# The constant of a recurrence as the bias column of its tanh, and bias rows as products over all 128 rows

## The chip, the cores and the metric

One NeuronCore of a Trainium2 chip runs the whole kernel. The metric is the device time of one execution in microseconds (us), the median of the runs shown. TensorE (PE) multiplies matrices, VectorE (DVE), ScalarE (ACT) and GpSimd (POOL) do the rest, and SyncE (SP) issues the DMAs.

## What is computed

The reference is two decoder layers on x of shape (8, 256, 128). What matters here is the second layer's state-space part and what comes right behind it:

```python
u  = einsum('bsd,nd->bsn', x, Wi) + bi
sp = einsum('bsd,nd->bsn', x, Ws) + bs
def step(state, inp):
    u_t, sp_t = inp
    state = tanh(state @ A.T + u_t @ B.T) + sp_t
    return (state, state @ C.T)
out = einsum('bsn,dn->bsd', ys, Wo) + bo        # ys: 256 steps, one after the other
x = layernorm(x + out)
x = layernorm(x + cross_attention(x, ctx))      # linear attention; its last step: att @ dense_w + dense_b
```

The first layer (local self-attention, cross-attention with rotary keys, a quantized product) comes before it and takes three quarters of the time. The last step of all is a quantized product with a normalization.

## The kernel before

**The recurrence.** The kernel keeps h_t = tanh(...) in place of the state. All batches are in one tile of 8 columns, so a step is `z_t = A h_(t-1) + (B Wi) x_t + (A Ws) x_(t-1) + constant`, then a tanh of 128 x 8. The part without h is put into PSUM (`cf`, four banks, 2048 columns) ahead of its step: the first 512 columns by `z_of` (L1776), the other 1536 in 12 blocks of 128 columns by `z_third` (L1791), one third of a block in each of the steps 1 to 36. The three thirds of a block are the product with x_t (`bwi_t`, L1798), the product with x_(t-1) (`aws_t`, L1801), and the constant (L1804). The constant is a row: `c_rows`, one partition of 256 values, multiplied by a row of ones (`one_row`, one partition), which puts the constant into every column. A product of one row is a matmul that contracts over one partition. In the trace its shape reads 1*64 (one row, 64 columns of weights), where the others read 128*64.

**A step.** On PE, `step(t)` (L1807) waits for `h_ready`, adds `A h` into the step's 8 columns by two matmuls of 64 output partitions each (L1810; an f32 matmul shows as two records, so one step shows as four) and raises `z_ready`. On ACT, `step(t)` (L900) waits for it, computes the tanh (L902, the first one L899) and raises `h_ready`. So the 256 steps are a chain that alternates between the two engines.

**What is woven in.** PE's instructions stand in one written-out order. Behind the matmuls of step t comes the work of `window(k, i)` (L1862) with k, i = divmod(t, 16): what the later parts need, cut into pieces of about one product. With 16 steps to a window of 128 tokens, piece 0 is `inputs_of`: the product with `gws_t` into `bank_d` and then the bias row (`one_row` times `bias_row`). Piece 1 is `states_of`, 2 to 5 the attention of an earlier window (`attend`, products of 16 columns), 6 is `dense` with its own bias row (`one_row` times one partition of `b_dense`), 7, 8, 11 and 15 are turns (L1818), 9 a product. `product_of_rows` (L1821) makes each as two halves of 64 partitions; its records are all on L1823, told apart by their operands: `x_t,sin_t` is `bias_row` with `one_row`, `b_dense,sin_t` the dense one. Where a step has no such piece, `keep_clock` (L1747) multiplies 192 columns (96 while there are thirds) that nobody reads.

**The small products.** Before the recurrence, PE makes the weight products (L1727 to L1738), among them the constants as rows of one partition: L1730, and L1735 to L1738, whose weights are single columns of `cols`. DVE copies them out (L1224, L1227, L1228). The tiles `bias_row`, `one_row` and `c_rows` are rows of `x_t`, `sin_t` and `rec_t`, free by then; POOL fills `one_row` at L681.

**The end.** SP's queue carries, for each window, a store of x4 and of the attention and a reload of the latter (L517, L521, L524), and behind those of window 13 eight loads (L531), then the rest for windows 14 and 15 and eight more loads (L535). The last sums on DVE wait for the loads.

Of the kernel before, what the change touches and what calls it, by code (L numbers as in the profile page):

```python
# [24 lines left out]
ACT = mybir.ActivationFunctionType  # L25
AX_X = mybir.AxisListType.X

B, T, D = 8, 256, 128
S = 512
P = 128  # L30
# [112 lines left out]
Z_FIRST = 512  # L143
Z_PARTS = (T * B - Z_FIRST) // P
# [3 lines left out]
KEEP, KEEP_Z = 192, 96  # L148
# [25 lines left out]
def decoder(nc, a, out):  # L174
    with ExitStack() as ctx:
        def sb(name, shape, dt=F32):
            return ctx.enter_context(nc.sbuf_tensor(name, shape, dt))

        def sem(name):
# [117 lines left out]
        x4_rows = bias_mask[:, :, :].rearrange("p h c -> p (h c)")[:, 0:WINDOWS * D].rearrange("p (t d) -> p t d", d=D)  # L297
        bias_row = x_t[0:1, 0:D]
        one_row = sin_t[0:1, :]
        c_rows = rec_t[0:1, 0:2 * D]  # L300
        t4 = cn[:, :, :]
# [3 lines left out]
        (F_MAX, F_SUM, F_ALL, BETA, INV_BETA, F_INV, F_SCALE, OUT_BIAS, Q_MAX, Q_SCALE, Q_INV) = (  # L305
            0, 4, 5, 6, 7, 8, 9, 10, 11, 13, 15)
        diag2 = sb("diag2", [2, 4])
        level = f_all
# [235 lines left out]
        def _(pool):  # L544
# [135 lines left out]
            pool.wait_ge(y_full, B)  # L680
            g.memset(one_row, 1.0).then_inc(ident16_ready, 1)  # L681
            norms = B * SELF_NORMS
# [50 lines left out]
        def _(act):  # L733
# [164 lines left out]
            act.wait_ge(c_ready, 1)  # L898
            s.activation(hid[:, 0:B], cf[:, 0:B], ACT.Tanh).then_inc(h_ready, 1)  # L899
            def step(t):  # L900
                act.wait_ge(z_ready, t)
                s.activation(hid[:, t * B:(t + 1) * B], cf[:, t * B:(t + 1) * B], ACT.Tanh).then_inc(h_ready, 1)  # L902

# [22 lines left out]
        def _(dve):  # L926
# [296 lines left out]
            w.tensor_copy(tail[:, 3:6, :].rearrange("p k d -> p (k d)"), bank_d[:, 0:3 * D])  # L1223
            w.tensor_copy(c_rows[:, 0:D], bank_d[0:1, 3 * D:4 * D]).then_inc(td_free, 1)  # L1224
            dve.wait_ge(td_full, 3)
            w.tensor_tensor(gws_t, bank_d[:, 0:D], ident[:, :], ALU.add)
            w.tensor_copy(c_rows[:, D:2 * D], bank_d[0:1, D:2 * D])  # L1227
            w.tensor_copy(bias_row, bank_d[0:1, 2 * D:3 * D]).then_inc(td_free, 1)  # L1228

# [176 lines left out]
        def _(pe):  # L1406
# [310 lines left out]
            for k in range(4):  # L1717
# [11 lines left out]
            mm(bank_d[:, 2 * D:3 * D], mats[:, M_C, :], wo_t, start=True, stop=True, skip_group_check=True)  # L1729
            mm(bank_d[0:1, 3 * D:4 * D], cols[:, BI_COL:BI_COL + 1], b_t, start=True, stop=True,  # L1730
               skip_group_check=True).then_inc(td_full, 1)

            pe.wait_ge(td_free, 2)
            mm(bank_d[:, 0:D], mats[:, M_WS, :], g_t, start=True, stop=True, skip_group_check=True)
            mm(bank_d[0:1, D:2 * D], cols[:, BI_COL:BI_COL + 1], b_t, start=True, stop=False, skip_group_check=True)  # L1735
            mm(bank_d[0:1, D:2 * D], cols[:, BS_COL:BS_COL + 1], a_t, start=False, stop=True, skip_group_check=True)
            mm(bank_d[0:1, 2 * D:3 * D], cols[:, BS_COL:BS_COL + 1], g_t, start=True, stop=False, skip_group_check=True)
            mm(bank_d[0:1, 2 * D:3 * D], cols[:, BO_COL:BO_COL + 1], ident[:, :], start=False, stop=True,  # L1738
               skip_group_check=True).then_inc(td_full, 1)

# [33 lines left out]
            pe.wait_ge(ta_free, 9)  # L1774
            pe.wait_ge(ident16_ready, 2)
            def z_of(lo, hi, start):  # L1776

                bank = cf[:, lo:hi]
                mm(bank, bwi_t, x3_t[:, lo:hi], start=start, stop=False, skip_group_check=True)
                skip = B if lo == 0 else 0  # L1780
                mm(bank[:, skip:], aws_t, x3_t[:, lo + skip - B:hi - B], start=False, stop=False,
                   skip_group_check=True)
                last = mm(bank[:, skip:], c_rows[:, D:2 * D], one_row[:, skip:hi - lo], start=False, stop=True,
                          skip_group_check=True)
                if skip:
                    last = mm(bank[:, 0:B], c_rows[:, 0:D], one_row[:, 0:B], start=False, stop=True,
                              skip_group_check=True)
                return last

            z_of(0, Z_FIRST, True).then_inc(c_ready, 1)  # L1790
            def z_third(part, third):  # L1791

                lo = Z_FIRST + P * part
                for half in range(0, P, HALF_ROWS):
                    of = slice(half, half + HALF_ROWS)
                    bank = cf[of, lo:lo + P]
                    if third == 0:
                        mm(bank, bwi_t[:, of], x3_t[:, lo:lo + P], start=(lo % 512 == 0), stop=False,  # L1798
                           skip_group_check=True)
                    elif third == 1:  # L1800
                        mm(bank, aws_t[:, of], x3_t[:, lo - B:lo + P - B], start=False, stop=False,  # L1801
                           skip_group_check=True)
                    else:
                        mm(bank, c_rows[:, D + half:D + half + HALF_ROWS], one_row[:, 0:P], start=False, stop=True,  # L1804
                           skip_group_check=True)
# [15 lines left out]
            def product_of_rows(bank, tokens, weights, **kw):  # L1821
                for of in halves:
                    last = mm(bank[of, 0:D], tokens[:, of], weights, skip_group_check=True, **kw)  # L1823
                return last

            def inputs_of(k):
                if k == 0:
                    pe.wait_ge(td_free, 9)
                else:
                    pe.wait_ge(q_ready, k)  # L1830
                product_of_rows(bank_d, x3_t[:, P * k:P * k + P], gws_t, start=True, stop=False)
                product_of_rows(bank_d, one_row[:, 0:P], bias_row, start=False, stop=False)

# [20 lines left out]
            def dense(k):  # L1854
                pe.wait_ge(mixed_t_ready, k + 1)
                if k >= 1:
                    pe.wait_ge(dense_normed, k)
                product_of_rows(bank_d2, mixed_t, w_dense[:, :], start=True, stop=False)
                product_of_rows(bank_d2, one_row[:, 0:P], b_dense[0:1, :], start=False,
                                stop=True).then_inc(dense_full, 1)  # L1860

# [38 lines left out]
            for t in range(1, T):  # L1900
                step(t)
                k, i = divmod(t, WINDOW_STEPS)
                worked = window(k, i)
                if t <= 3 * Z_PARTS:
                    z_third(*divmod(t - 1, 3))
                if not worked:
                    keep_clock(KEEP_Z if t <= 3 * Z_PARTS else KEEP, bank_d2 if t < Z_FIRST // B else sc[:, 0, :])
            pe.wait_ge(h_ready, T)
# [56 lines left out]
```

## Time and profile before

| | |
|---|---|
| median of 3 runs | 1149.36 us (1147.28 to 1156.16) |
| the profiled execution's own time | 1147.91 us |
| its span, first to last instruction | 1146.1 us |
| mean granted clock of TensorE | 0.889 of full speed |
| the recurrence, first tanh (L899) to last | 901.6 to 1075.4 us |
| tanh instructions L902 | 255, each 0.177 us |
| steps 1 to 248, 902.20 to 1070.88 us | 168.68 us, mean granted clock 0.79 |

How to read it: times count from the span's first instruction. The granted clock is 1.00 or 0.50 at any moment (2.4 or 1.2 GHz); a mean between them is a share of time. In a timeline row, the bracket says how long the engine stood idle before, and who released it.

### The profile page before, as it was taken

The page shows a single profiled execution, that of the slowest core. Times are in us where ns is not written, and L with a number is a line of the kernel's source. Part 1 is how long each engine was busy: PE and PEld are TensorE (multiplying, and loading weights), DVE is VectorE, ACT ScalarE, POOL GpSimd, SP SyncE. Part 2 cuts the span into 40 slices and gives each one's busy share as a digit, 9 for nine tenths or more (in the row PEclk, how much of TensorE's full clock was granted, in tenths as well). Part 3 has the DMA queues.
Part 4 walks back from the last instruction along what each step waited for, and adds up shares of the span by engine and source line. Part 5 has one row for each costly group of instructions (what it writes and reads, how often), then busy time and mean ns, then how long its engine had stood idle before and what let it go on. Part 6 is the DMA issues. An engine that isn't in the chain of part 4 may idle for free.

```text
span 1146.1 us, 21485 instructions
## 1 busy us (share of the span) xinstructions
PE 966.1 (84%) x8233; PEld 665.1 (58%) x8233; DVE 682.3 (60%) x1923; ACT 500.3 (44%) x1412; POOL 494.0 (43%) x615
## 2 busy tenths in 40 slices
PE   3658999998999999899899999988844899999811
PEld 2435666666665666666666575655533677677501
DVE  3356676657657766875776777575555123433478
ACT  3636654563564565466456455633310222332200
POOL 1035366356446545644644654566531012222351
PEclk8689999999899999999999999999975877877755
DMA  6000000000000000000000000000000011111400
GB/s 175 20 1 6 11 1 5 11 1 5 2 10 1 5 11 1 6 11 1 1 5 11 2 1 1 2 1 20 1 1 0 4 16 18 20 23 18 54 7 37
DMA packets 60396, 15.06 MB, mean 13 GB/s; under 512 B 41334, under 2 KB 59526, under 8 KB 60166
## 3 DMA queue, kind: packets, MB, share of 16 engines
q1 hardware_dynamic: 60294, 13.69, 6.0%
q8 instruction: 66, 1.08, 0.4%
q14 instruction: 36, 0.29, 0.1%
HBM read 10.51 MB, written 3.17 MB: 12 GB/s over the span
## 4 chain that ended last, share of the span: by engine, by line
PE 61%; DVE 20%; ACT 6%; POOL 5%; issue 3%; SPq 3%; DMA 2%; POOLq 0%; DVEq 0%
PE score_banks L1650 8%; PE out_bank L1622 7%; PE bank_a L1410 5%; PE score_banks L1429 5%; PE score_banks L1810 5%; DVE o_rec L1130 5%; DVE prob L1158 3%; PE score_banks L1454 3%; PE bank_d L1505 3%; PE score_banks L1431 3%; PE out_bank L1605 3%; PE score_banks L1430 3%; PE bank_d L1823 3%; PE out_bank L1630 2%; PE score_banks L1749 2%
## 5 line engine op out<-in xcount | busy, mean ns | idle before, releaser
L851 ACT ACTIVATE prob<-score_banks 128x1024 f32<-128x1024 f32 x128 | 131.0, 1023 | 166.0 <-PE score_banks L1650 165.8
L1650 PE MATMUL score_banks<-qh,kr 64*128 64x256 f32 x1024 | 149.6, 412 | 3.1 <-ACT qh L819 2.7
L664 POOL TENSOR_TENSOR psum<-psum,prob 128x512 f32<-128x512 f32 x64 | 81.6, 1276 | 156.7 <-DVE prob L1158 156.7
L1130 DVE RECIPROCAL o_rec<-out_bank 128x256 f32<-128x256 f32 x64 | 111.9, 1748 | 30.6 <-PE out_bank L1630 30.6
L662 POOL TENSOR_TENSOR psum<-prob 128x512 f32<-128x512 f32 x64 | 83.0, 1297 | 102.6 <-DVE prob L1158 102.6
L1622 PE MATMUL out_bank<-prob,v 128*64 128x256 f32 x1024 | 124.7, 386 | 1.3 <-DVE on L1131 1.3
L1650 PEld LDWEIGHTS score_banks<-qh,kr 64*128 64x128 f32 x1024 | 91.2, 191 | 41.8 <-issue 32.4
L791 ACT ACTIVATE prob<-prob,neg_max 128x128 f32<-128x128 f32 (+1 forms) x256 | 107.1, 426 | 12.9 <-DVE neg_max L1030 12.9
L1158 DVE TENSOR_SCALAR prob<-prob 128x1024 f32<-128x1024 f32 x128 | 101.2, 791 | 18.4 <-ACT prob L851 18.4
L902 ACT ACTIVATE prob<-score_banks 128x8 f32<-128x8 f32 x255 | 45.2, 177 | 121.5 <-PE score_banks L1810 121.5
L1622 PEld LDWEIGHTS out_bank<-prob,v 128*64 128x64 f32 x1024 | 67.8, 136 | 46.6 <-issue 17.2
L1810 PE MATMUL score_banks<-prob,pt 128*64 128x8 f32 x1020 | 89.7, 228 | 1.8 <-ACT prob L899 0.3
L1810 PEld LDWEIGHTS score_banks<-prob,pt 128*64 128x64 f32 x1020 | 68.1, 163 | 38.8 <-ACT prob L902 27.1
L1092 DVE TENSOR_TENSOR k_cos<-score_banks,cos_t 128x512 f32<-128x512 f32 x56 | 38.2, 682 | 82.1 <-PE score_banks L1431 45.9
L640 POOL TENSOR_TENSOR kr<-k_cos,k_sin 128x512 f32<-128x512 f32 x64 | 82.8, 1294 | 8.8 <-DVE k_sin L1094 8.7
L666 POOL TENSOR_TENSOR psum<-psum,prob 128x512 f32<-128x512 f32 x64 | 81.5, 1273 | 3.9
L1505 PE MATMUL bank_d<-km,q 64*128 64x128 f32 (+1 forms) x512 | 57.4, 346 | 24.4 <-DVE row_max L1025 21.0
L742 ACT ACTIVATE pt<-bank_a 128x512 f32<-128x512 f32 x96 | 57.3, 597 | 42.9 <-PE bank_a L1410 41.8
L690 POOL TENSOR_TENSOR var_eps<-mv,epsilons 128x1 f32<-128x1 f32 x48 | 9.1, 189 | 149.8 <-DVE mv L1276 149.8
L1410 PE MATMUL bank_a<-ident,prob 128*128 128x128 f32 x384 | 62.3, 286 | 11.6 <-ACT pt L742 5.4
L1410 PEld LDWEIGHTS bank_a<-ident,prob 128*128 128x128 f32 x384 | 43.1, 142 | 33.5 <-ACT pt L742 17.6
L1505 PEld LDWEIGHTS bank_d<-km,q 64*128 64x128 f32 x512 | 37.3, 203 | 40.8 <-issue 39.0
(340 smaller groups left out, 2114.3 us busy)
## 6 DMA issues: line engine op xcount, KB each, us to landing
cb<-in_ctx_dram SPq DMA_DIRECT2D x8, 256.0 KB, 2.8
bias_mask<-bias_scratch SPq DMA_DIRECT2D x1, 1536.0 KB, 7.4
xb<-in_x_dram SPq DMA_DIRECT2D x8, 128.0 KB, 2.1
prob<-in_L_xattn_Wkv_dram SPq DMA_DIRECT2D x1, 1024.0 KB, 7.1
x_scratch<-v SPq DMA_DIRECT2D x16, 64.0 KB, 1.5
att_scratch<-on SPq DMA_DIRECT2D x16, 64.0 KB, 1.5
prob<-att_scratch SPq DMA_DIRECT2D x16, 64.0 KB, 2.9
out_dram<-v SPq DMA_DIRECT2D x4, 256.0 KB, 2.5
```

Of the source, the lines that this page charges most:

```text
L640: g.tensor_tensor(kr[:, key % 2, :], k_cos[:, :], k_sin[:, :], ALU.add).then_inc(kr_ready, 1)
L662: link(g.tensor_tensor(psum[:, p % 2, :], pp[:, 0, :], pp[:, 1, :], ALU.add))
L664: link(g.tensor_tensor(psum[:, p % 2, :], psum[:, p % 2, :], pp[:, 2, :], ALU.add))
L791: last = s.activation(pr, pr, ACT.Exp, bias=neg_max[:, qt, j, g:g + 1], accum_out=row_sum[:, qt, j, g:g + 1])
L851: s.activation(prob[:, p % 2, 2 * u:2 * u + 2, :].rearrange("p k (h q) -> p h k q", h=2), sc[:, 0:2, :].rearrange("p h (k q) -> p h k q", ...
L1130: link(w.reciprocal(o_rec[:, :], bank[:, T:2 * T]))
L1158: w.tensor_scalar(pr, pr, float(np.exp(-CLIP)), float(np.exp(CLIP)), ALU.max, ALU.min).then_inc(clamped, 1)
L1410: return nc.tensor.transpose(out_ap, in_ap, ident[0:in_ap.shape[0], 0:in_ap.shape[0]])
L1505: last = mm(bank[:, lo:lo + k.stop - k.start], q0[rows_of, q], km[rows_of, jj, k], start=True, stop=True, skip_group_check=True)
L1622: mm(o[DH * h:DH * (h + 1), 0:T], v[:, (q // 2) % 2, kb, lo:lo + DH], prob[:, q % 2, kb, T * h:T * (h + 1)], start=(kb == 0), stop=(kb == ...
L1650: last = mm(sc[:, h, k * T:(k + 1) * T], kr[rows_of, p % 2, kb * P:(kb + 1) * P], qh[rows_of, p % 2, :], start=True, stop=True, skip_group ...
L1810: last = mm(cf[lo:lo + HALF_ROWS, t * B:(t + 1) * B], a_t[:, lo:lo + HALF_ROWS], hid[:, (t - 1) * B:t * B], start=False, stop=True, skip_g ...
```

## The change

The constant of the recurrence is no longer multiplied into PSUM. It is kept as a column of 128 values (`z_bias`: one column for the first step, one for the others), made by products with one moving column, and given to the tanh as its bias. The thirds become halves: 12 blocks in the steps 1 to 24, `keep_clock` with 192 columns from step 25 on. The two bias rows of the side work stay products, but over all 128 rows: `first_row` is a 128 x 64 tile whose first partition is ones and the rest zeros; `pre_bias` holds the bias row on all 128 partitions (its weights are a column broadcast over 128 columns), and `b_dense` was loaded on all partitions already.

```diff
-        bias_row = x_t[0:1, 0:D]
-        one_row = sin_t[0:1, :]
-        c_rows = rec_t[0:1, 0:2 * D]
+        pre_bias = x_t[:, 0:D]
+        first_row = rec_t[:, 0:HALF_ROWS]
+        z_bias = sb("z_bias", [P, 2])
 ...
             pool.wait_ge(y_full, B)
-            g.memset(one_row, 1.0).then_inc(ident16_ready, 1)
 ...
             act.wait_ge(c_ready, 1)
-            s.activation(hid[:, 0:B], cf[:, 0:B], ACT.Tanh).then_inc(h_ready, 1)
+            act.wait_ge(td_free, 3)
+            s.activation(hid[:, 0:B], cf[:, 0:B], ACT.Tanh, bias=z_bias[:, 0:1]).then_inc(h_ready, 1)
             def step(t):
                 act.wait_ge(z_ready, t)
-                s.activation(hid[:, t * B:(t + 1) * B], cf[:, t * B:(t + 1) * B], ACT.Tanh).then_inc(h_ready, 1)
+                s.activation(hid[:, t * B:(t + 1) * B], cf[:, t * B:(t + 1) * B], ACT.Tanh,
+                             bias=z_bias[:, 1:2]).then_inc(h_ready, 1)
 ...
-            w.tensor_copy(c_rows[:, 0:D], bank_d[0:1, 3 * D:4 * D]).then_inc(td_free, 1)
+            w.tensor_copy(z_bias[:, 0:1], bank_d[:, 3 * D:3 * D + 1])
+            w.tensor_copy(first_row, ident[:, 0:1].broadcast_to([P, HALF_ROWS])).then_inc(td_free, 1)
 ...
-            w.tensor_copy(c_rows[:, D:2 * D], bank_d[0:1, D:2 * D])
-            w.tensor_copy(bias_row, bank_d[0:1, 2 * D:3 * D]).then_inc(td_free, 1)
+            w.tensor_copy(z_bias[:, 1:2], bank_d[:, D:D + 1])
+            w.tensor_copy(pre_bias, bank_d[:, 2 * D:3 * D]).then_inc(td_free, 1)
 ...
-            mm(bank_d[0:1, 3 * D:4 * D], cols[:, BI_COL:BI_COL + 1], b_t, start=True, stop=True,
+            mm(bank_d[:, 3 * D:3 * D + 1], b_t, cols[:, BI_COL:BI_COL + 1], start=True, stop=True,
                skip_group_check=True).then_inc(td_full, 1)
 ...
-            mm(bank_d[0:1, D:2 * D], cols[:, BI_COL:BI_COL + 1], b_t, start=True, stop=False, skip_group_check=True)
-            mm(bank_d[0:1, D:2 * D], cols[:, BS_COL:BS_COL + 1], a_t, start=False, stop=True, skip_group_check=True)
-            mm(bank_d[0:1, 2 * D:3 * D], cols[:, BS_COL:BS_COL + 1], g_t, start=True, stop=False, skip_group_check=True)
-            mm(bank_d[0:1, 2 * D:3 * D], cols[:, BO_COL:BO_COL + 1], ident[:, :], start=False, stop=True,
-               skip_group_check=True).then_inc(td_full, 1)
+            mm(bank_d[:, D:D + 1], b_t, cols[:, BI_COL:BI_COL + 1], start=True, stop=False, skip_group_check=True)
+            mm(bank_d[:, D:D + 1], a_t, cols[:, BS_COL:BS_COL + 1], start=False, stop=True, skip_group_check=True)
+            to_all = [P, P]
+            mm(bank_d[:, 2 * D:3 * D], cols[:, BS_COL:BS_COL + 1].broadcast_to(to_all), g_t, start=True, stop=False,
+               skip_group_check=True)
+            mm(bank_d[:, 2 * D:3 * D], cols[:, BO_COL:BO_COL + 1].broadcast_to(to_all), ident[:, :], start=False,
+               stop=True, skip_group_check=True).then_inc(td_full, 1)
 ...
-                last = mm(bank[:, skip:], c_rows[:, D:2 * D], one_row[:, skip:hi - lo], start=False, stop=True,
-                          skip_group_check=True)
-                if skip:
-                    last = mm(bank[:, 0:B], c_rows[:, 0:D], one_row[:, 0:B], start=False, stop=True,
-                              skip_group_check=True)
-                return last
+                return mm(bank[:, skip:], aws_t, x3_t[:, lo + skip - B:hi - B], start=False, stop=True,
 ...
-                        mm(bank, c_rows[:, D + half:D + half + HALF_ROWS], one_row[:, 0:P], start=False, stop=True,
 ...
+            def bias_of_rows(bank, row, **kw):
+                for of in halves:
+                    last = mm(bank[of, 0:D], first_row, row, skip_group_check=True, **kw)
+                return last
 ...
-                product_of_rows(bank_d, one_row[:, 0:P], bias_row, start=False, stop=False)
+                bias_of_rows(bank_d, pre_bias, start=False, stop=False)
 ...
-                product_of_rows(bank_d2, one_row[:, 0:P], b_dense[0:1, :], start=False,
-                                stop=True).then_inc(dense_full, 1)
+                bias_of_rows(bank_d2, b_dense[:, :], start=False, stop=True).then_inc(dense_full, 1)
 ...
-                if t <= 3 * Z_PARTS:
-                    z_third(*divmod(t - 1, 3))
+                if t <= 2 * Z_PARTS:
+                    z_half(*divmod(t - 1, 2))
                 if not worked:
-                    keep_clock(KEEP_Z if t <= 3 * Z_PARTS else KEEP, bank_d2 if t < Z_FIRST // B else sc[:, 0, :])
+                    keep_clock(KEEP_Z if t <= 2 * Z_PARTS else KEEP, bank_d2 if t < Z_FIRST // B else sc[:, 0, :])
```

## Rows read from the trace of the kernel before

**Rows 1.** The page, part 2: granted clock of TensorE in 40 slices of 28.65 us.

```profile
PEclk8689999999899999999999999999975877877755
```

**Rows 2.** Waits of ScalarE in the recurrence, 901 to 1076 us.

```profile
ACT prob L902 <- PE score_banks L1810: 121.5, 255, 1.3
```

**Rows 3.** Chain that ended last, from 1071 us (start, us, what).

```profile
1074.17 1.04 SPq L531
```

**Rows 4.** Timeline of one step, first weaving part, full clock (start, us, engine ...).

```profile
903.21 0.43 PE L1804 MATMUL score_banks<-sin_t,rec_t 1*64 1x128 f32 x4
903.33 0.18 ACT L902 ACTIVATE prob<-score_banks 128x8 f32<-128x8 f32 x1 [0.39 <-PE score_banks L1810]
...
904.07 0.18 ACT L902 ACTIVATE prob<-score_banks 128x8 f32<-128x8 f32 x1 [0.57 <-PE score_banks L1810]
```

**Rows 5.** Timeline of a side product step at full clock.

```profile
989.86 0.18 ACT L902 ACTIVATE prob<-score_banks 128x8 f32<-128x8 f32 x1 [0.39 <-PE score_banks L1810]
...
990.01 0.43 PE L1823 MATMUL bank_d<-x_t,sin_t 1*64 1x128 f32 x4
...
990.71 0.18 ACT L902 ACTIVATE prob<-score_banks 128x8 f32<-128x8 f32 x1 [0.67 <-PE score_banks L1810]
```

**Rows 6.** Timeline of a side product step at the low clock.

```profile
966.73 0.18 ACT L902 ACTIVATE prob<-score_banks 128x8 f32<-128x8 f32 x1 [0.49 <-PE score_banks L1810]
...
968.19 0.18 ACT L902 ACTIVATE prob<-score_banks 128x8 f32<-128x8 f32 x1 [1.28 <-PE score_banks L1810]
...
968.86 0.18 ACT L902 ACTIVATE prob<-score_banks 128x8 f32<-128x8 f32 x1 [0.49 <-PE score_banks L1810]
```

**Rows 7.** Timeline of step 17: two 128-row products, full clock.

```profile
912.44 0.42 PE L1823 MATMUL bank_d<-pt,prob 128*64 128x128 f32 x4
...
912.64 0.18 ACT L902 ACTIVATE prob<-score_banks 128x8 f32<-128x8 f32 x1 [0.89 <-PE score_banks L1810]
912.69 0.39 PE L1801 MATMUL score_banks<-prob,pt 128*64 128x128 f32 x4
...
913.20 0.18 ACT L902 ACTIVATE prob<-score_banks 128x8 f32<-128x8 f32 x1 [0.39 <-PE score_banks L1810]
```

**Rows 8.** Timeline of two keep-clock steps, low clock.

```profile
930.84 0.18 ACT L902 ACTIVATE prob<-score_banks 128x8 f32<-128x8 f32 x1 [0.68 <-PE score_banks L1810]
...
931.69 0.18 ACT L902 ACTIVATE prob<-score_banks 128x8 f32<-128x8 f32 x1 [0.68 <-PE score_banks L1810]
```

**Rows 9.** Groups of ScalarE by form: mean ns of one, without and with operand columns.

```profile
L742 ACT ACTIVATE ctx_t<-bank_a,cols 128x512 f32<-128x512 f32 x8 | 6.2, 773 | 7.5 <-PE bank_a L1410 7.5
...
L742 ACT ACTIVATE ctx_t<-bank_a 128x512 f32<-128x512 f32 x8 | 4.8, 602 | 0.0
...
L738 ACT ACTIVATE sin_t<-bank_a,sign 128x512 f32<-128x512 f32 x1 | 0.7, 687 | 0.0
```

**Rows 10.** Timeline of the first constants of the recurrence.

```profile
899.43 1.01 PE L1781 MATMUL score_banks<-prob,pt 128*128 128x504 f32 x2
...
901.63 0.18 ACT L899 ACTIVATE prob<-score_banks 128x8 f32<-128x8 f32 x1 [3.22 <-PE score_banks L1786]
```

**Rows 11.** Timeline of the weight products, 858 to 865 us.

```profile
858.96 0.64 PE L1728 MATMUL bank_d<-pt,km 128*128 128x128 f32 x2
...
859.39 0.64 PE L1729 MATMUL bank_d<-pt,km 128*128 128x128 f32 x2
...
861.37 0.80 PE L1734 MATMUL bank_d<-pt,km 128*128 128x128 f32 x2 [0.84 <-DVE rec_t L1224]
...
862.10 0.58 PE L1735 MATMUL bank_d<-pt,cols 128*1 128x128 f32 x2
```

**Rows 12.** Busy time, clock and DMA of three windows of 16 steps.

```profile
989.86:1000.31 10.45, 10.32 (x152) 7.17 (x148) 4.31 (x16) 3.34 (x19) 3.09 (x8) 0.84 0.16 20
1021.01:1032.28 11.27, 11.14 (x150) 8.40 (x148) 4.07 (x16) 3.35 (x20) 3.09 (x8) 0.71 0.16 21
966.73:979.38 12.65, 12.64 (x152) 9.51 (x150) 4.36 (x16) 3.34 (x19) 3.09 (x8) 0.56 0.13 17
```

More of the change, by code:

```diff
@@ L1774, in _ @@
             pe.wait_ge(ta_free, 9)
-            pe.wait_ge(ident16_ready, 2)
+            pe.wait_ge(ident16_ready, 1)
             def z_of(lo, hi, start):
@@ L1780, in z_of, with z_half @@
                 skip = B if lo == 0 else 0
-                mm(bank[:, skip:], aws_t, x3_t[:, lo + skip - B:hi - B], start=False, stop=False,
-                   skip_group_check=True)
-                last = mm(bank[:, skip:], c_rows[:, D:2 * D], one_row[:, skip:hi - lo], start=False, stop=True,
+                return mm(bank[:, skip:], aws_t, x3_t[:, lo + skip - B:hi - B], start=False, stop=True,
                           skip_group_check=True)
-                if skip:
-                    last = mm(bank[:, 0:B], c_rows[:, 0:D], one_row[:, 0:B], start=False, stop=True,
-                              skip_group_check=True)
-                return last
             z_of(0, Z_FIRST, True).then_inc(c_ready, 1)
-            def z_third(part, third):
+            def z_half(part, which):
                 lo = Z_FIRST + P * part
@@ L1796, in z_third @@
                     bank = cf[of, lo:lo + P]
-                    if third == 0:
+                    if which == 0:
                         mm(bank, bwi_t[:, of], x3_t[:, lo:lo + P], start=(lo % 512 == 0), stop=False,
                            skip_group_check=True)
-                    elif third == 1:
-                        mm(bank, aws_t[:, of], x3_t[:, lo - B:lo + P - B], start=False, stop=False,
-                           skip_group_check=True)
                     else:
-                        mm(bank, c_rows[:, D + half:D + half + HALF_ROWS], one_row[:, 0:P], start=False, stop=True,
+                        mm(bank, aws_t[:, of], x3_t[:, lo - B:lo + P - B], start=False, stop=True,
                            skip_group_check=True)
```

## The prediction, made before the changed kernel ran

> **What bounds the kernel now.** I read the page first. The granted clock is nearly full until slice 30 and then 0.5 to 0.8 [rows 1]: something else begins there, at about 900 us, and that is the recurrence, the part that the change touches. Next the waits of ScalarE there. All 255 tanh waited for PE, 121.5 us together [rows 2], and PE's next step waits for the tanh in turn. So neither engine is the bound by its load; a chain through both is, one link per step. In the timeline I took the distance from tanh to tanh in each of the 247 intervals between step 1 and step 248 (168.68 us), and sorted them by what PE had in them:
>
> - 114 plain ones at the full clock, 0.565 us each. PE's side work is hidden: even with two products over 128 rows the interval is 0.56 [rows 7].
> - 54 plain ones at the low clock, 0.666 (968.19 to 968.86 in [rows 6]).
> - 32 at the low clock with `keep_clock` of 192 columns, 0.853 [rows 8]. These are bound by PE, not by the chain.
> - 8 in between (the clock changed in them).
> - 39 with a product of one row. 10 are those of the thirds, 0.747 [rows 4]; steps 16 and 32 take 1.06 and 1.07, steps 33 and 36 0.85 and 0.82. 25 are in `inputs_of` and `dense` from step 48 on: 20 at 0.850 [rows 5], 4 at 1.46 (966.73 to 968.19 in [rows 6]), one of 1.05.
>
> The one-row product costs time though it moves no more columns than the others: 0.285 us more than a plain interval in rows 5, where a second product over 128 rows costs nothing in rows 7.
>
> Last the end of the chain: SP's loads L531 start at 1074.17 [rows 3], behind the attention of window 13, which step 248 carries. From there the chain is SP's and DVE's own. So what happens up to step 248 moves the end one to one, and what happens behind it on PE (the bias rows of the last windows too) is hidden behind SP's eight loads.
>
> **The bias column on the tanh.** It adds no instruction, but each tanh reads a column of SBUF that it did not read before. No row shows a tanh with one. The nearest rows: the same evacuation of 128x512 costs 602 ns with no column, 773 with scale and bias columns, and 687 with a scale column alone [rows 9]. So one column is 85 ns (687 - 602) and two are 171. The row with one column stood alone and waited for PE before it, as the tanh does, so the wait did not hide it. Bounds: 0, if the column is fetched while the instruction waits; 0.11 as the upper end, the price of rows 9 and a quarter more. I take 0.087, what one column costs there (0.085) rounded up. Where the chain bounds, it is paid in full. Where `keep_clock` bounds it is free, since 0.853 - 0.666 = 0.187 covers it. Plain intervals become 0.652 and 0.753.
>
> The Trainium skill says the same against this change. In ScalarE: Activation LUTs, under What ACT_TABLE_LOAD costs, each [128,1] pointer operand adds about 93 ns to an activation with immediates. By that price the sum below would be 1.0 us higher (an estimate: 168 plain intervals times 6 ns); the rows above have the price for other functions and agree within 10%.
>
> **Interval by interval, at the clock pattern of the trace:**
>
> - 114 + 54 = 168 plain, +0.087 each: +14.6.
> - 32 with `keep_clock`: 0. The 8 mixed ones, about +0.04 each: +0.3.
> - Steps 25 to 36 now have `keep_clock` with 192 columns and no third: 0, hidden by the chain while the clock is full, as in the plain ones; 0.1 each (0.853 - 0.753) if the clock falls there.
> - 10 thirds, 0.747 to 0.652: -0.95.
> - Step 16 has two side products and one half, three products. Two take 0.25 us apart (912.44 and 912.69 [rows 7]) and fit 0.56, so three end near 0.8: -0.25. Step 32 no longer has a half: 1.07 to 0.652, -0.4. Steps 33 and 36: -0.35 together.
> - 20 side biases, 0.850 to 0.652 (two 128-row products fit): -4.0.
> - 4 at the low clock. 128 columns take 0.25 at the full clock, so 0.50 here. `keep_clock` with 192 columns makes 0.853 [rows 8]; two products are 256 columns, 64 more, so 0.853 + 0.25 = 1.10 (an estimate). 1.46 to 1.10 is -1.4 for the four, and the mixed one -0.25. The ends are 0.753 (all hidden) and 1.46 (nothing gained), so -2.8 and 0.
>
> Sum: +14.9 - 7.6 = +7.3.
>
> **Ahead of the recurrence.** `z_of` loses its constants: L1781 ends at 900.44, the first tanh started at 901.63 [rows 10]. That is -1.15, and +0.09 for its own bias column. The first tanh's new wait (`td_free` 3) is for copies of the products that ran at about 862 [rows 11], so it is long met, and PE waits for one POOL instruction less. The weight products: two 128-wide ones start 0.43 apart, but the first one-column product starts 0.73 after L1734 [rows 11]. I put that gap down to the change of shape, which goes twice: -0.6. The added copy of `first_row` (64 columns) stands between two links on DVE: +0.1. Range of the two -1.0 to +0.5, since a 128-column load of a broadcast column has no row. POOL's memset goes at a time when POOL next waits for DVE's statistics, which hide it: 0, and if they did not, a gain of under 1 us. Together -1.56.
>
> At the same clock pattern the sum is +7.3 - 1.56 = +5.7 us.
>
> **The clock.** It falls for short stretches in each window, after the attention's 16-column products, and that is dear: a window of 16 steps took 10.45 at a mean clock of 0.84, 11.27 at 0.71, 12.65 at 0.56 [rows 12], so 0.8 us for one low stretch more (10.45 to 11.27). The change pulls both ways. The same columns are spread over longer steps, which would let it fall more often; and the one-row products become products of the whole array, which would let it fall less often. The trace has no row for either. Longer steps are 168 of 247, bias products 25, so I lean to the first: two or three more low stretches, +2. Bounds -3 and +7.
>
> Result: +5.7 + 2 = +7.7 on the profiled execution's own 1147.91 (its span of 1146.1 and 1.8 around it), so 1155.6. The median of the runs is 1.45 above that execution, so 1149.36 + 7.7 = 1157.1.
>
> **The rivals.**
> 1. *The column is fetched during the wait* (faster). Place: each tanh. For it: the instruction is queued well before its data. Against: rows 9. The time: thirds 10 x 0.18, steps 16, 32, 33 and 36 together 1.3, 20 x 0.285, 4 x 0.36 and 0.45 for the mixed one make -10.7; -1.65 ahead of the recurrence; shorter steps with the same columns would also keep the clock up, -2. 1149.4 - 14.3 = 1135.1. It is faster by over 1% up to a column of (14.3 - 11.5) / 168 = 0.017 us.
> 2. *The clock stays down more* (clearly slower). Place: windows 3 to 15, where the attention's small products stand in longer steps; the window at 0.56 shows how far it can go [rows 12]. With eight more low stretches it is 8 x 0.8 = +6.4 in place of +2: 1149.4 + 5.7 + 6.4 = 1161.5. From eight on it is over 1%.
> 3. *The clock gains*, since bias products of the whole array keep it up: three fewer low stretches, -2.5: 1149.4 + 5.7 - 2.5 = 1152.6.
> 4. *The one-row penalty does not go*: if it came from adding a bias to a bank that was just written and not from the row count, the steps keep 0.85 + 0.087. Against it: a third's constant (another bank, other operands) is late in the same way [rows 4]. The 25 side steps would lose their gain again, 25 x 0.285: 1149.4 + 5.7 + 7.1 = 1162.2.
>
> **How the numbers follow.** A measurement of this kernel can tell about 1% (11.5 us) from no change. Forecast 1157.1: 0.45. Rival 1: 0.13. Rival 2: 0.22. Rival 3: 0.15. Rival 4: 0.05. Faster by over 1% is rival 1, 0.13. Slower by over 1% is rivals 2 and 4 and a tail of the forecast, 0.29. The rest, 0.58, is within 1%, most of it above the old time. The range for 8 in 10 reaches from rival 3 with part of a cheaper column, 1145, to rival 2 with a column of 0.1, 1167.
>
> **What would show it.** In the changed profile: tanh rows of about 0.264 us, not 0.177; plain intervals 0.65; no shape 1*64, and side bias steps at the full clock equal to plain ones; the low-clock ones near 1.10; the first tanh 1.1 us after L1781's place, not 2.2. Tanh rows of 0.177, or intervals of 0.565 in spite of a longer tanh, would make the forecast wrong and rival 1 right. A mean clock below 0.75 over the recurrence would be rival 2, above 0.82 rival 3.

## The result and the profile after

| | before | changed |
|---|---|---|
| median of 15 runs each | 1149.67 us (1140.25 to 1156.16) | 1158.43 us (1155.05 to 1160.11) |
| profiled execution's span | 1146.1 us | 1156.7 us |
| first tanh to step 1's tanh start | 901.63 to 902.20 | 899.60 to 900.25 |
| steps 1 to 248 | 168.68 us, clock 0.79 | 181.36 us, clock 0.75 |

The ratio is 1.0062, with a 95% interval of 1.0039 to 1.0085: slower by 0.4 to 0.9%. The forecast was 1157.1 us.

The page's clock line of the changed kernel answers to [rows 1]. In slices 32 to 38, which lie in the recurrence, it reads 9676777 where it read 8778777. (The first slices differ too, long before anything that was changed.)

```profile
PEclk9979999999999899999999999998965967677755
```

The group of the tanh in the lines by form. It was 177 ns; it reads a third operand now, `z_bias`, and takes 267 ns:

```profile
L902 ACT ACTIVATE prob<-score_banks,z_bias 128x8 f32<-128x8 f32 x255 | 68.2, 267 | 112.3 <-PE score_banks L1805 112.3
```

So the column costs 90 ns in the instruction. What the chain makes of it, in the timeline at a step with a side product and its bias row, at the full clock; it answers to [rows 5], where the interval was 0.85:

```profile
968.26 0.27 ACT L902 ACTIVATE prob<-score_banks,z_bias 128x8 f32<-128x8 f32 x1 [0.39 <-PE score_banks L1805]
968.31 0.39 PE L1823 MATMUL bank_d<-x_t,rec_t 128*64 128x128 f32 x4
...
968.92 0.27 ACT L902 ACTIVATE prob<-score_banks,z_bias 128x8 f32<-128x8 f32 x1 [0.39 <-PE score_banks L1805]
```

The shape 1*64 is gone, the bias row reads 128*64, and the interval is 0.66, which is also what a plain step takes (0.565 before). Plain intervals: about 126 of the 247 at 0.65 or 0.66, and 52 at 0.76 at the low clock (0.666 before). Six with two products at the low clock take 1.07, where [rows 6] had 1.46. One of them in the timeline:

```profile
960.28 0.27 ACT L902 ACTIVATE prob<-score_banks,z_bias 128x8 f32<-128x8 f32 x1 [0.46 <-PE score_banks L1805]
...
960.54 0.65 PE L1823 MATMUL bank_d<-b_dense,rec_t 128*64 128x128 f32 x4
...
961.35 0.27 ACT L902 ACTIVATE prob<-score_banks,z_bias 128x8 f32<-128x8 f32 x1 [0.63 <-PE score_banks L1805]
```

The first constants answer to [rows 10]. The tanh starts 1.05 us behind the start of the product with `aws_t` (L1781 before, L1785 now), where it was 2.20:

```profile
898.55 1.01 PE L1785 MATMUL score_banks<-prob,pt 128*128 128x504 f32 x2
...
899.60 0.27 ACT L899 ACTIVATE prob<-score_banks,z_bias 128x8 f32<-128x8 f32 x1 [2.06 <-PE score_banks L1785]
```

The weight products answer to [rows 11]. The product with one moving column, L1732, starts 0.42 behind L1731, and L1737 0.59 behind L1736 where the one-column weights had needed 0.73. From the sum product (L1724 before, L1726 now, at 857.70 and 857.36) to DVE's next reduction it took 6.91 us before (864.61) and takes 6.37 now:

```profile
859.05 0.63 PE L1731 MATMUL bank_d<-pt,km 128*128 128x128 f32 x2
...
859.47 0.42 PE L1732 MATMUL bank_d<-cols,pt 128*128 128x1 f32 x2
...
860.72 0.80 PE L1736 MATMUL bank_d<-pt,km 128*128 128x128 f32 x2 [0.82 <-DVE rec_t L1226]
...
861.31 0.42 PE L1737 MATMUL bank_d<-cols,pt 128*128 128x1 f32 x2
...
863.73 0.68 DVE L1234 TENSOR_REDUCE small<-prob 128x1 f32<-128x512 f32 x1
```

Two windows of 16 steps, and steps 1 to 248 as a whole, with TensorE's clock behind the bracketed counts; they answer to [rows 12]. Nearly all windows from step 80 on take 11.70 and 12.20 by turns, with the same places at the low clock each time, while before they varied from 10.3 to 12.65:

```profile
956.06:968.26 12.20, 11.60 (x152) 8.62 (x152) 4.44 (x16) 4.78 (x19) 3.07 (x8) 0.70 0.13 17
968.26:979.96 11.70, 11.00 (x150) 7.86 (x148) 4.16 (x16) 4.78 (x19) 3.09 (x8) 0.73 0.14 18
900.25:1081.61 181.36, 172.40 (x2300) 125.85 (x2298) 58.53 (x203) 72.72 (x288) 39.24 (x104) 0.75 0.12 17
```

A mean clock of 0.75 says how long the low clock held: 2 x (1 - 0.75) x 181.36 = 91 us; before, with 0.79, it was 71. The clock is read to two decimals, so such a figure is good to about 2 us.

And the end, SP's first load L531, answers to [rows 3]. It starts 10.73 us later than before, which is the whole difference of the spans (10.6); nothing was gained or lost behind it:

```profile
1084.90 1.05 SPq L531
```

### The profile page after: what moved, and what is told of

Read it like the earlier page. It is cut to its first block, busy times and chain, and to the rows that moved or that the text cites. A ratio compares the mean times of both kernels' runs of the same rounds, so it can differ in the third digit from the quotient of the medians.

```text
span 1156.7 us, 21383 instructions
## 1 busy us (share of the span) xinstructions
PE 970.0 (84%) x8181; PEld 668.8 (58%) x8181; DVE 682.5 (59%) x1924; ACT 523.1 (45%) x1412; POOL 493.1 (43%) x614
## 4 chain that ended last, share of the span: by engine, by line
PE 61%; DVE 19%; ACT 8%; POOL 4%; issue 3%; SPq 3%; DMA 2%; POOLq 0%; DVEq 0%
PE score_banks L1652 9%; PE out_bank L1624 7%; PE score_banks L1805 5%; PE bank_a L1412 5%; PE score_banks L1431 5%; DVE o_rec L1131 4%; DVE prob L1159 3%; PE score_banks L1456 3%; PE bank_d L1507 3%; PE score_banks L1432 3%; PE score_banks L1433 3%; PE out_bank L1607 3%; PE score_banks L1753 2%; PE out_bank L1632 2%; ACT prob L902 2%
## 5 line engine op out<-in xcount | busy, mean ns | idle before, releaser
L902 ACT ACTIVATE prob<-score_banks,z_bias 128x8 f32<-128x8 f32 x255 | 68.2, 267 | 112.3 <-PE score_banks L1805 112.3
```

## The experiments

Two theories stood against each other after the result. **Theory:** the column is paid on the chain, the rows are saved on PE, and both prices are those of the intervals plus what they do to the clock. **Rival:** the clock alone makes the difference, or the saving of the rows isn't there. The two parts of the change are taken apart first, then the clock is held.

### e1: the column alone

```diff
+            act.wait_ge(td_free, 3)
+            s.activation(hid[:, 0:B], cf[:, 0:B], ACT.Tanh, bias=z_bias[:, 0:1]).then_inc(h_ready, 1)
...
+                s.activation(hid[:, t * B:(t + 1) * B], cf[:, t * B:(t + 1) * B], ACT.Tanh,
+                             bias=z_bias[:, 1:2]).then_inc(h_ready, 1)
...
+            w.memset(z_bias[:, :], 0.0)
```

> The kernel before with one thing added: each tanh gets a bias column, which is zero (a DVE memset makes it). Theory (the column costs about 0.09 us in every step whose interval the chain sets): tanh rows of 0.267 us; plain intervals 0.656 at the full and 0.757 at the low clock; the intervals with keep_clock at the low clock stay 0.853 and those with a one-row side product 0.85, because PE sets them. 168 x 0.09 = +15, and 2 to 4 more by low clock: 1149.7 + 18 = 1168. Rival (the time of the changed kernel comes from the clock alone, and the column is fetched beside the chain): the same within 3 us of before, 1150.

Measured: 1182.95 us (1180.54 to 1184.70), ratio 1.0298 (1.0262 to 1.0335). The group of its tanh (the 230 that ran before 1090 us), and a window of 16 steps with steps 1 to 248:

```profile
L904 ACT ACTIVATE prob<-score_banks,z_bias 128x8 f32<-128x8 f32 x230 | 61.6, 268 | 119.4 <-PE score_banks L1814 119.4
```

```profile
974.25:988.23 13.98, 13.98 (x150) 10.03 (x150) 4.28 (x16) 4.78 (x20) 3.10 (x8) 0.50 0.12 15
902.55:1104.21 201.66, 197.94 (x2348) 140.08 (x2346) 58.31 (x203) 72.81 (x288) 39.65 (x104) 0.64 0.11 15
```

The row of the tanh is as the theory had it, and so are the intervals: 0.656 at the full clock, 0.753 to 0.760 at the low one, 0.853 with `keep_clock`, and 0.85 for one-row steps. But the total is 33.3 above before, not 18. The clock is why: it is 0.64 over steps 1 to 248, 145 us at the low clock in place of 71, and six of the windows are wholly at 0.50 and take 13.98. The rival falls. The theory's direct price stands, and its price for the clock (2 to 4 us) was far too small.

### e2 and e3: the rows without the column

e2 is the changed kernel with the tanh's column off (it leaves out the constant):

```diff
-                s.activation(hid[:, t * B:(t + 1) * B], cf[:, t * B:(t + 1) * B], ACT.Tanh,
-                             bias=z_bias[:, 1:2]).then_inc(h_ready, 1)
+                s.activation(hid[:, t * B:(t + 1) * B], cf[:, t * B:(t + 1) * B], ACT.Tanh).then_inc(h_ready, 1)
```

> The changed kernel with the bias column taken off the tanh, all else as changed (it leaves out the constant of the recurrence). Theory: plain intervals back to 0.565 and 0.666, side steps at the full clock 0.565 too; 10.7 us saved in the steps, 2 ahead of them, 2 by the clock: 1149.7 - 14.7 = 1135. Rival (the clock alone): as the changed kernel, 1158.

e3 computes everything. It is the kernel before, with every one-row product made one of 128 rows:

```diff
+            link(g.memset(first_ones[:, :], 0.0))
+            g.memset(first_ones[0:1, :], 1.0).then_inc(ident16_ready, 1)
...
+            mm(bank_d[:, 3 * D:4 * D], cols[:, BI_COL:BI_COL + 1].broadcast_to(to_all), b_t, start=True, stop=True,
...
-                        mm(bank, c_rows[:, D + half:D + half + HALF_ROWS], one_row[:, 0:P], start=False, stop=True,
+                        mm(bank, c_all[:, D + half:D + half + HALF_ROWS], first_ones[:, 0:P], start=False, stop=True,
```

> A version that takes the product over 128 rows for all constants, those of the recurrence too, and leaves the tanh without a column: the thirds stay thirds, their constant is c_all (the constant on all partitions) with a tile whose first partition is ones. Theory: a third's constant hides in the 0.565 of its step as the other two thirds do, so it is as fast as e2 plus about 1 us for the first 512 columns' constant ahead of the recurrence: 1136. Rival (each side product that is left in costs something, whatever its rows): the 12 thirds keep their 0.18, so 1139 or more.

Measured: e2 1126.41 us (ratio 0.9814, 0.9779 to 0.9849), e3 1123.63 us (0.9779, 0.9746 to 0.9812). They are 8.6 and 12.4 below what was expected. A window and the steps 1 to 248 of e3:

```profile
978.34:987.39 9.05, 8.89 (x152) 6.08 (x150) 4.23 (x16) 3.35 (x20) 3.10 (x8) 1.00 0.17 23
903.88:1048.21 144.33, 142.44 (x2348) 106.04 (x2346) 57.61 (x203) 50.63 (x287) 39.29 (x103) 0.93 0.15 21
```

A window in which the clock never falls takes 16 x 0.565 = 9.05, with both bias rows in it: they are hidden wholly. The thirds' intervals are 0.56 and 0.57 in e3, so the rival of e3 falls: a third's constant over 128 rows costs nothing there. Here too the saving is larger than expected (26 us, not 14), and here too it is the clock: 0.93, 20 us at the low clock in place of 71.

### e4: the side products alone

Against e3, the constants of the recurrence (this line, and the two of `z_of`) go back to one row:

```diff
-                        mm(bank, c_all[:, D + half:D + half + HALF_ROWS], first_ones[:, 0:P], start=False, stop=True,
+                        mm(bank, c_all[0:1, D + half:D + half + HALF_ROWS], first_ones[0:1, 0:P], start=False, stop=True,
```

> As e3, but the constants of the recurrence stay products of one row; only the bias rows of the side products (inputs_of, dense) are over 128 rows. It splits the saving. Theory: thirds' intervals 0.747 again, 1.8 us for the ten and 0.8 for steps 18 to 36 with side work, so 1139; the side steps 0.565 at the full clock. Rival (the one-row penalty sits in the thirds alone): 1149.

Measured: 1128.15 us (ratio 0.982, 0.9788 to 0.9853). The thirds' intervals are 0.75 and the side steps 0.565, as the theory had them; the total was expected at 1139 and is 11 below it, with a mean clock of 0.90 over steps 1 to 248. So of e3's 26 us, 21.5 come from the two bias rows per window and 4.5 from the recurrence's own constants.

### e7, e8, e9, e12: the same square with the clock held

If the clock carries so much, then holding it must leave the direct prices. Before it falls PE has the attention's steps, with products of 16 columns only; so these four kernels get a product of 128 columns there that nobody reads (the fill):

```diff
                 worked = window(k, i)
+                if 2 <= i <= 5 and 0 <= k - 2 < WINDOWS and t > 2 * Z_PARTS:
+                    keep_clock(P, bank_d2 if t < Z_FIRST // B else sc[:, 0, :])
```

(3 * Z_PARTS in e8, e9 and e12, which have thirds.)

> The changed kernel, with a keep_clock product of 128 columns added behind each of the attention's steps (pieces 2 to 5) once the halves are through; nobody reads it. It asks how much of the column's price is the clock. Theory (0.09 us per tanh directly, the rest because longer steps let the clock fall in the attention's steps): the clock stays near full over steps 1 to 248, all intervals 0.656, 247 x 0.656 = 162.2 us where the changed kernel took 181.4: 1158.4 - 19 = 1139. Rival (the clock does not depend on these steps): low stretches stay, and the added work costs up to 0.1 in each attention step at the low clock, 1158 to 1162.

> e3 (all constants over 128 rows, no column) with the same fill. Theory: full clock, 247 x 0.565 + 0.4 = 140 us where e3 took 144.3: 1123.6 - 4 = 1119.5; against e7 it is the column's direct price alone, 247 x 0.09 = 22. Rival (clock not to be held): 1124 to 1127.

> The kernel before with the same fill. Theory: at the full clock 208 x 0.565 + 10 x 0.747 + 25 x 0.85 + 3.8 = 150 us where before took 168.7: 1149.6 - 18.7 = 1131; against e8 it is the direct price of the one-row products alone, 10 to 11. Rival (it is the one-row products that let the clock fall, however much else PE does): the clock still falls in most windows, 1145 to 1155.

> e1 (the kernel before with a zero column on each tanh) with the fill. It completes the square at the full clock: e8 (128 rows, no column), e9 (one row, no column), e7 (128 rows, column), and this (one row, column). Theory (where a one-row product makes PE late, it covers the column; everywhere else the column is paid whole): intervals 0.656, the thirds' constants 0.745, side steps 0.85 as without the column; 1131.6 + 208 x 0.09 = 1150, so that the rows are worth only 7 here (against e7, 1143) where they are worth 10.6 without the column. Rival (the two prices add): 1131.6 + 22 = 1153.6, 10.6 above e7.

Measured: e7 1143.04 us (ratio 0.9935, 0.9906 to 0.9964), e8 1121.00 (0.9746, 0.9709 to 0.9784), e9 1131.60 (0.9833, 0.9794 to 0.9872), e12 1156.53 (1.0080, 1.0053 to 1.0107). The windows of steps 80 to 96, then steps 1 to 248, of e7, e8, e9 and e12 in this order:

```profile
954.09:964.62 10.53, 9.97 (x160) 6.52 (x158) 4.23 (x16) 4.79 (x19) 3.06 (x8) 1.00 0.16 20
902.03:1064.70 162.67, 155.16 (x2414) 103.50 (x2410) 57.75 (x203) 72.89 (x287) 39.28 (x103) 1.00 0.14 19
```

```profile
947.89:957.06 9.17, 9.12 (x160) 6.54 (x158) 4.22 (x16) 3.35 (x20) 3.07 (x8) 1.00 0.11 20
902.40:1044.27 141.87, 141.28 (x2456) 105.67 (x2452) 57.54 (x203) 50.61 (x287) 39.13 (x103) 1.00 0.16 21
```

```profile
951.84:961.57 9.73, 9.69 (x160) 6.49 (x156) 4.22 (x16) 3.35 (x19) 3.07 (x8) 1.00 0.10 19
902.59:1054.41 151.82, 151.22 (x2456) 105.16 (x2452) 57.56 (x203) 50.63 (x288) 39.26 (x103) 1.00 0.15 20
```

```profile
957.40:968.31 10.91, 10.36 (x160) 6.48 (x156) 4.23 (x16) 4.79 (x20) 3.08 (x8) 1.00 0.06 15
902.79:1082.69 179.90, 174.03 (x2456) 117.33 (x2452) 57.79 (x203) 72.87 (x287) 39.45 (x104) 0.90 0.13 17
```

In three of them the clock stays at 1.00 over steps 1 to 248. So what PE does in those steps decides whether the clock falls, and the windows give the prices without it. In e12 it still fell in three windows (0.90), where the filled steps then take 1.07 and 1.28 us. Its total is therefore no direct price: it is 6.5 above what was expected and 13.5 above e7, which is nearer to the rival's 10.6 than to the theory's 7. Only its full-clock windows (10.91) decide for the theory.

| one window of 16 steps, full clock | one-row | 128 rows | rows worth |
|---|---|---|---|
| no column | 9.73 (e9) | 9.17 (e8) | 0.56 |
| column | 10.91 (e12) | 10.53 (e7) | 0.38 |
| column costs | 1.18 | 1.36 | |

0.56 is two side steps at 0.28; 0.38 is two at 0.19, since 0.85 - 0.656 is all that is left to gain. The prices don't add: the late PE covers the column in the steps where it is late. The fill covers it in one step too: the attention's last piece takes 0.685 with the fill, with or without a column, so a window without the fill would pay 0.09 more for the column. The totals give e7 - e8 = 22.0 for the column at 128 rows and e9 - e8 = 10.6 for the rows without it; steps 1 to 248 of the profiles give 20.8 and 10.0. The parts ahead of the recurrence differ by some us between executions (the first tanh of e5 starts at 896.6, that of e3 at 903.3), so the steps are the closer measure.

### e5 and e11: what makes the one-row product late

The line of `inputs_of`; that of `dense` is changed in the same way:

```diff
-                product_of_rows(bank_d, first_ones[:, 0:P], pre_bias[:, :], start=False, stop=False)
+                product_of_rows(bank_d, first_ones[0:64, 0:P], pre_bias[0:64, :], start=False, stop=False)     # e5, on e3
+                mm(bank_d[:, 0:D], first_ones[:, 0:P], pre_bias[:, :], start=False, stop=False, ...)           # e11, on e8
```

> As e3, but the bias rows of inputs_of and dense are products over 64 rows, no longer 1 or 128. It asks what makes the one-row product late. Theory (the change of the shape in which the array is used, for which 64 rows is another shape than 128): the side steps take 0.85 at the full clock as with one row, so 25 x 0.285 = 7 more than e3 and more by the clock, 1131 to 1146. Rival (one row is slow in itself, a matmul over many rows is not): as e3, 1124.

> As e8, but the bias rows of inputs_of and dense are each one product with 128 columns of weights, no longer two halves of 64; the rows stay 128. Theory (what costs is the change between shapes of the array's use, in columns as in rows): the side steps take about 0.85 again, 25 x 0.28 = 7 more: 1128. Rival (only a change in the number of rows costs): the one product of 128 columns takes 0.25 as the two halves do, intervals 0.57 to 0.6, 1121 to 1122.

Measured: e5 1142.89 us (ratio 0.9946, 0.9921 to 0.9971), e11 1129.22 (0.9836, 0.9789 to 0.9883). A side step at the full clock in the timeline, first of e5, then of e11, then the same weight load before (one row) and in e3 (128 rows):

```profile
957.70 0.18 ACT L903 ACTIVATE prob<-score_banks 128x8 f32<-128x8 f32 x1 [0.39 <-PE score_banks L1815]
957.85 0.20 PEld L1828 LDWEIGHTS bank_d<-x_t,sin_t 64*64 64x64 f32 x4 [0.17 <-issue]
...
958.56 0.18 ACT L903 ACTIVATE prob<-score_banks 128x8 f32<-128x8 f32 x1 [0.67 <-PE score_banks L1815]
```

```profile
958.61 0.18 ACT L903 ACTIVATE prob<-score_banks 128x8 f32<-128x8 f32 x1 [0.39 <-PE score_banks L1815]
958.75 0.30 PEld L1837 LDWEIGHTS bank_d<-x_t,sin_t 128*128 128x128 f32 x2 [0.17 <-issue]
...
959.51 0.18 ACT L903 ACTIVATE prob<-score_banks 128x8 f32<-128x8 f32 x1 [0.73 <-PE score_banks L1815]
```

```profile
990.01 0.19 PEld L1823 LDWEIGHTS bank_d<-x_t,sin_t 1*64 1x64 f32 x4 [0.17 <-issue]
```

```profile
978.29 0.25 PEld L1828 LDWEIGHTS bank_d<-x_t,sin_t 128*64 128x64 f32 x4
```

With 64 rows the interval is 0.86 (957.70 to 958.56), as with one row; with the whole width in one product it is 0.90. In e5, e11 and before, the load of the bias row's weights starts only after 0.17 of idle time; in e3 it has none. So 128 rows alone do not make the product free (e11), and a single row is not needed to make it late (e5). What the late ones have in common is that the array is used in another shape than by the products before and behind, which are all 128 rows by 64 columns. The time is lost on both sides: from the product with `gws_t` to the bias row 0.35 (989.66 to 990.01) where e3 takes 0.24 (978.15 to 978.39), and from there to the next `A h` 0.37 where e3 takes 0.22. More columns to stream is not what makes e11 late: a whole-width product of 504 columns is followed by the next 0.85 later in e8 below, so 128 columns take an estimated 0.21, no more than the 0.25 of two halves [rows 7]. The Trainium skill has a rule for this, in TensorEngine Tiling (Array Packing), under Key Properties: "Changing tiling mode (not just tile) drains the TensorE". The page lists 128x128, 128x64 and 64x64 as such modes, so e5 and e11 agree with it; of a single row it says nothing. The rows put a price on it, 0.28 to 0.34 us at the full clock for going there and back.

Not all of a one-row product's lateness is shown to be that. In `z_of` two one-row products follow each other, without a change of shape, and the second starts 0.95 behind the first (before, first fence); the same two over 128 rows start 0.85 apart (e8, second fence). That 0.10 is open.

```profile
900.36 1.11 PE L1783 MATMUL score_banks<-sin_t,rec_t 1*128 1x504 f32 x2
...
901.31 0.28 PE L1786 MATMUL score_banks<-sin_t,rec_t 1*128 1x8 f32 x2
```

```profile
900.66 1.01 PE L1788 MATMUL score_banks<-sin_t,rec_t 128*128 128x504 f32 x2
...
901.51 0.28 PE L1791 MATMUL score_banks<-sin_t,rec_t 128*128 128x8 f32 x2
```

e5 also differs from e3 in the clock, 0.79 over steps 1 to 248 where e3 has 0.93:

```profile
897.14:1064.37 167.23, 165.49 (x2350) 122.79 (x2346) 57.70 (x203) 50.63 (x288) 39.24 (x103) 0.79 0.13 18
```

### e6: two columns

On e7:

```diff
+                             bias=z_bias[:, 1:2], scale=ones[:, 0:1]).then_inc(h_ready, 1)
```

> e7 (the changed kernel, filled) with a second column on each tanh: a scale column of ones. Theory (each column adds about 0.09 us to the tanh, and the chain pays it whole): tanh rows 0.357 us, intervals 0.746 in place of 0.656, 247 x 0.09 = 22 more: 1143 + 22 = 1165. Rival (the first column's price is one fetch that a second shares): as e7, 1143 to 1148.

Its four runs took 1163.56, 1164.68, 1185.08 and 1189.17 us, with a mean clock over the whole kernel of 0.93, 0.92, 0.89 and 0.88. The ratio of 1.0141 (1.0081 to 1.0200) is that of the first two, near the 1165 expected; the profile is of the third. Here the fill did not hold the clock: it is 0.73 over steps 1 to 248. The group of its tanh in the lines by form (the 169 that ran before 1040 us):

```profile
L902 ACT ACTIVATE prob<-score_banks,z_bias,ones 128x8 f32<-128x8 f32 x169 | 60.5, 358 | 76.7 <-PE score_banks L1805 76.7
```

358 ns: 91 more than with one column, 181 more than with none. Its plain intervals at the full clock are 0.747. Each column is a price of its own, paid whole.

### e10: a version meant to beat both

On e8, with the constants of the first 512 columns ahead of the last input product:

```diff
-            for _ in range(8):
+            pe.wait_ge(ident16_ready, 2)
+            mm(cf[:, 0:B], c_all[:, 0:D], first_ones[:, 0:B], start=True, stop=False, skip_group_check=True)
+            mm(cf[:, B:Z_FIRST], c_all[:, D:2 * D], first_ones[:, B:Z_FIRST], start=True, stop=False,
+               skip_group_check=True)
+            for _ in range(5):
                 keep_clock()
...
-            z_of(0, Z_FIRST, True).then_inc(c_ready, 1)
+            z_of(0, Z_FIRST, False).then_inc(c_ready, 1)
...
+                    keep_clock(P if i < 5 else HALF_ROWS, bank_d2 if t < Z_FIRST // B else sc[:, 0, :])
```

> A version to beat both. e8 with two more edits: the constants of the first 512 columns go into PSUM before the last input product is ready, in the place of 3 of the 8 keep_clock products, so that z_of has two products only; and the fill behind the attention's last piece is 64 columns, not 128, since that step took 0.69. Theory: 1.1 us from z_of, up to 1 from the keep_clock products, 13 x 0.12 = 1.5 from the attention's last pieces: 1121.0 - 3.5 = 1117.5. Rival (with fewer keep_clock products the clock is low where z_of runs, and what is saved is lost there): 1121 or more.

Measured: 1120.06 us (1117.30 to 1120.84), ratio 0.9753 (0.9721 to 0.9786), against e8's 0.9746. In the timeline:

```profile
892.75 1.80 PE L1777 MATMUL score_banks<-sin_t,rec_t 128*128 128x504 f32 x2
...
899.97 1.01 PE L1789 MATMUL score_banks<-prob,pt 128*128 128x504 f32 x2
...
901.02 0.18 ACT L900 ACTIVATE prob<-score_banks 128x8 f32<-128x8 f32 x1 [2.06 <-PE score_banks L1789]
```

The constants' product runs at 892.75, in time that `keep_clock` filled, and the first tanh starts 1.05 behind the start of `z_of`'s last product (e8: 2.01). The attention's last piece takes 0.58, not 0.69, and steps 1 to 248 take 140.46 us (e8: 141.87). The spans differ by 1.6 (1116.8 and 1118.4) in its favour, the medians by 0.9, and the intervals of the two ratios overlap. So it is 2.5% faster than before. 1117.5 was expected; that it is faster than e8 is likely by its intervals and not settled by the runs.

## Why the prediction was right

**The column** was sized from [rows 9] at 0.087; the tanh row and the plain interval show 0.090 and 0.091. One reading behind it was wrong. The row with one column (L738, 687 ns) did not wait for PE: [rows 9] gives it 0.0 of idle time, it stood right behind a table load that had waited. That a wait does not hide the fetch could have been read from two other groups of the trace before, where two columns cost 180 ns behind long waits:

```profile
L742 ACT ACTIVATE x_t<-bank_a,cols 128x256 f32<-128x256 f32 x8 | 4.5, 564 | 46.9 <-PE bank_a L1410 46.9
...
L742 ACT ACTIVATE x_t<-bank_a 128x256 f32<-128x256 f32 x8 | 3.1, 384 | 1.4 <-PE bank_a L1410 0.8
```

Rival 1 (fetched during the wait) is excluded by e1, e2 and e6. The price that the Trainium skill gives in ScalarE: Activation LUTs, under What ACT_TABLE_LOAD costs, 93 ns for each pointer operand, agrees with the 90 and 91 of these rows.

**The covers** held: intervals with `keep_clock` at the low clock stayed 0.853 with the longer tanh, so the column was free there. Side steps at the full clock went from 0.85 to 0.656 as forecast, the low ones to 1.07 (estimate 1.10), step 16 to 0.77 (estimate 0.8).

**Ahead of the recurrence** -1.56 was forecast; the first tanh came 2.03 earlier, of which 0.54 are the weight products (forecast -0.5), 1.15 the constants of `z_of`, and 0.34 was there before the first changed instruction. (Part of the forecast's -1.56 was +0.09 for the first tanh's own column; it shows in the distance to step 1, 0.65 where it was 0.57.)

**The end.** That step 248 moves the end one to one held to 0.1 us.

**The clock** is the term that was mis-sized. Steps 1 to 248 took 12.7 us longer (168.68 to 181.36) where the sum at the old clock pattern had +7.3; the column at 0.091 and not 0.087 is 0.7 of the difference (168 x 0.004), so about 4.7 are the clock, where +2 was forecast with bounds of -3 and +7. The low clock went from 71 to 91 us. The prediction took 0.8 us for one low stretch more from two windows of [rows 12], but each of these has one stretch: they differ by 3.2 us in its length (2 x 0.16 x 10.45 = 3.3 and 2 x 0.29 x 11.27 = 6.5). 20 us more are six times that, not two or three. The stretches did not become many more (13 before, 14 after, counted in the intervals) but longer. With a mean of 0.75 the profile stands on the mark that was set for rival 2.

**Luck** is in how close the total came. The profiled executions differ by 10.5 us (1147.91 and 1158.43) where 7.7 was forecast. The medians differ by 8.8, because the median before lies 1.8 above its profiled execution and the one after does not.

**Two large clock terms** stand behind the small net, and the prediction sized neither. By the medians, the column costs 34.8 us at 128 rows (changed kernel against e3), of which 22.0 are direct and 12.8 remain for the clock; the rows save 26.0 (e3 against before), 10.6 direct and 15.4 the clock. Steps 1 to 248 of the profiles split as 37.0 = 20.8 + 16.2 and 24.4 = 10.0 + 14.4. So each clock term is 12 to 16 us, where the prediction moved between -3 and +7, and they nearly cancel (-2.6 by the medians, +1.8 by the steps; the direct prices are here those at the full clock throughout). Low stretches also got cheaper in themselves: the column is free in the 0.853 intervals, and none costs 1.46 any more. The same error shows in rival 1's number: it gave 1135.1 for a change without the column's price, and e2 and e3 took 1126.4 and 1123.6.

**Rival 3** (bias products of the whole array keep the clock up) was true of the rows taken alone, and outweighed by the column. **Rival 4** is excluded by e3 and e4.

**Open:** what in the one-row steps lets the clock fall. It may be the wait of PE around the change of shape, or the longer step. e5 shows only that 64 rows are as bad for it as one (0.79 both), so it isn't the single row; e11, over all 128 rows, had the fill and can't tell. Open is also why the fill held the clock in e7 and e9 and not in three windows of e12 nor in the profile of e6: the steps of e12 are longer than those of e9, but those of e7 are too.

## What to carry to other kernels

- In a chain between two engines a column operand of the instruction in the chain is latency in each link: here 0.09 us x 247 steps outweighed all that the constant and both bias rows had cost on TensorE (22 against 10.6 at the full clock). Put a constant where an engine has slack.
- Small products between others should have their shape. Padding one row to 128 made it free in steps with room for a second product, and 64 rows did not.
- Before trading work between engines, look at what the low clock costs in that stage and hold the clock once by a fill: it gives the direct prices, and here the fill alone was worth 1.7% (e9). Look in the profile whether it held: in e12 and e6 it did not, and a filled step at the low clock took 1.07 to 1.28 us.

## What the runs showed of the hardware that was not expected

- Changing one part of a step by 0.09 or 0.28 us moved the time by 1.6 to 2.5 times its direct price (34.8 against 22.0 for the column, 26.0 against 10.6 for the rows) through TensorE's clock: 145 us at the low clock (1.2 GHz) in e1, 71 before, 20 in e3, and none in e7, e8 and e9, with the same useful work in each.
- With the unread product in four of 16 steps the clock stayed at 2.4 GHz over steps 1 to 248 (1.00 in e7 and e9), where the mean had been 0.79 (before) and 0.75 (changed); in e12 (0.90) and e6 (0.73) it did not.
- A product over 64 rows between products over 128 is as late as one over a single row (0.86 and 0.85), and one over 128 rows in the whole width later still (0.90).
